# Twelve sorted batches for ten, gates spread by TensorE for gates read from memory, row numbers read for two rounds at once, and every store on ScalarE's queue

## The reference

```
x2   = layernorm(src);  sel = sigmoid(x2 @ sel_w)            # 32 scores
scores, idx = top_k(sel, 4);  gate = scatter of scores       # 28 of 32 gates are zero
h    = relu(einsum("bsd,edh->bseh", x2, keys))
out  = src + einsum("bseh,ehd,bse->bsd", h, values, gate)
```

## Time and profile before

| | |
|---|---|
| median of three executions | 2879.79 us |
| profiled execution, its own time | 2882.87 us |
| its span | 2880.8 us |
| PE busy | 2593.1 us (90%) |
| DVE busy | 1998.2 us (69%) |
| ACT busy | 1546.8 us (54%) |
| POOL busy | 1537.2 us (53%) |
| mean granted TensorE clock | 0.963 |

### The profile page before, as it was taken

The page is one execution under the profiler, slowest core; times in us unless marked ns, Lnnn a source line. Parts: engine busy times, 40 slices in busy tenths (PEclk is TensorE's granted clock), DMA queues, the critical chain, the costliest instruction groups (busy, mean ns, idle before and its releaser), DMA issues. The chain is left out here.

```text
span 2880.8 us, 60293 instructions
## 1 busy us (share of the span) xinstructions
PE 2593.1 (90%) x19992; PEld 1974.2 (69%) x19992; DVE 1998.2 (69%) x4720; ACT 1546.8 (54%) x4605; POOL 1537.2 (53%) x2150
## 2 busy tenths in 40 slices
PE   7999798799979999999886989998999999989699
PEld 5888576588858777777772446665877777769344
DVE  5554587455458999998653556775899999866254
ACT  2333344233359888888510016776988888862000
POOL 4333664432246888887206324554678888740550
PEclk9999899899979999999998989998999999999799
DMA  3700465610022222223264455552222222225454
GB/s 115 312 1 1 112 142 116 261 46 1 1 54 48 54 59 60 60 60 109 67 177 138 174 154 121 107 117 51 45 51 60 60 60 59 55 79 167 147 191 137
DMA packets 225620, 275.90 MB, mean 96 GB/s; under 512 B 26099, under 2 KB 194291, under 8 KB 211987
## 3 DMA queue, kind: packets, MB, share of 16 engines
q1 hardware_dynamic: 190882, 240.03, 30.5%
q0 software_dynamic: 10240, 20.99, 2.6%
q10 hardware_dynamic: 24192, 11.02, 1.3%
HBM read 145.40 MB, written 122.22 MB: 93 GB/s over the span
## 5 line engine op out<-in xcount | busy, mean ns | idle before, releaser
L2803 ACT ACTIVATE f4a_pr<-f4a_sr,f4a_nm 128x256 f32<-128x256 f32 x512 | 239.1, 479 | 50.5 <-DVE f4a_nm L2869 50.2
L2803 ACT ACTIVATE f6a_pr<-f6a_sr,f6a_nm 128x256 f32<-128x256 f32 x512 | 239.0, 479 | 48.0 <-DVE f6a_nm L2869 47.7
L3006 POOL TENSOR_TENSOR f4a_rr<-a5b_room 128x256 f32<-128x256 f32 x256 | 195.3, 763 | 96.1 <-DVE a5b_room L2877 90.1
L3006 POOL TENSOR_TENSOR f6a_rr<-a5b_room 128x256 f32<-128x256 f32 x256 | 195.0, 762 | 87.5 <-DVE a5b_room L2877 81.7
L2005 DVE TENSOR_REDUCE a_nm<-a_sr 128x2 f32<-128x512 f32 x256 | 166.7, 684 | 70.8 <-PE a_sr L1738 69.8
L2877 DVE TENSOR_TENSOR a5b_room<-f4a_ur,f4a_turn 128x512 f32<-128x512 f32 x256 | 174.2, 681 | 35.4 <-PE f4a_ur L2663 33.5
L2877 DVE TENSOR_TENSOR a5b_room<-f6a_ur,f6l_turn 128x512 f32<-128x512 f32 x256 | 174.2, 681 | 30.6 <-PE f6a_ur L2663 27.8
L2869 DVE TENSOR_REDUCE f4a_nm<-f4a_sr 128x2 f32<-128x512 f32 x256 | 174.8, 683 | 20.2 <-PE f4a_sr L2680 19.4
L2678 PE MATMUL f4a_sr<-f4a_pe_hi,f4a_rr_hi 128*128 128x256 f32 x512 | 187.9, 367 | 0.0
L2869 DVE TENSOR_REDUCE f6a_nm<-f6a_sr 128x2 f32<-128x512 f32 x256 | 174.8, 683 | 18.9 <-PE f6a_sr L2680 18.2
L2678 PE MATMUL f6a_sr<-f6l_pe_hi,f6a_rr_hi 128*128 128x256 f32 x512 | 187.5, 366 | 0.0
(11 more groups left out here) (620 smaller groups left out, 8359.4 us busy)
## 6 DMA issues: line engine op xcount, KB each, us to landing
slots<-f_zero SPq DMA_DIRECT2D x84, 512.0 KB, 5.9
f4m_gate<-f4m_gates SPq DMA_DIRECT2D x24, 1024.0 KB
f6m_gate<-f6m_gates SPq DMA_DIRECT2D x24, 1024.0 KB
f4m_xr<-slots SPq DMA_DIRECT2D x112, 64.0 KB, 1.9
f6m_xr<-slots SPq DMA_DIRECT2D x112, 64.0 KB, 1.9
r_scratch<-r_parts SPq DMA_DIRECT2D x32, 192.0 KB, 2.3
all_qs<-r_scratch SPq DMA_DIRECT2D x16, 384.0 KB, 4.8
all_ks<-r_scratch SPq DMA_DIRECT2D x16, 384.0 KB, 6.7
```

The source lines that it names most:

```text
L2803: last = nc.scalar.activation(pr[:, n % 4, x, :], sr.bank(b, n)[:, x * T:(x + 1) * T], ACT.Exp, bias=nm[:, n % SB, x:x + 1], accum_out=zs[ ...
L3006: nc.gpsimd.tensor_tensor(rr[:, hs % RAW, :], tmp[:, hs % 2, 0, :], tmp[:, hs % 2, 1, :], ALU.add)\
```

## The change

- SENT is 12: 24 tiles of tokens are sorted, TILES = 128, ROUNDS = 32, SHARE = 3072, `slots` grows from 86016 to 102400 rows (50 clearing DMAs in each routed feed-forward). Two groups stay for the dense part, N = 64. The table of tiles is made one step later (steps 17 and 18).
- Gates aren't stored and read any more. DVE splits the gates of a group into three bf16 parts (`split`, after rounds 6 and 8), PE turns the three parts together (rounds 9 and 12), and in the dense part PE multiplies a column of ones and zeros (`expert`) by them (`spread`, bf16, 96 rows, 512 columns), which gives the gate of one expert on all partitions; ACT copies it (`take_gate`, 128 x 512), and `weigh` reads the copy. `kept_ps` has two banks instead of three, `gate_ps` two.
- Row and expert numbers are read for two rounds at a time, eight numbers.
- All four stores of a round are ACT's.
- `mix` comes at products 9, 14, 20, 25, 31, 36, 42, 47, 53, 58 and, for the last two, after the loop. The stores of the output come after the rounds in another order on SP.

```diff
-SENT = 10
+SENT = 12
+PARTS = 3
...
-                if it[0] == B and n == 0:
+                if it[0] == B + 1 and n == 0:
                     opening.sort_counts(pe, fill(it, "counts")).then_inc(desk.filled, 1)
...
-                if it[0] == B + 1 and n == 0:
+                if it[0] == B + 2 and n == 0:
                     opening.sort_turn(pe, fill(it, "table")).then_inc(desk.filled, 1)
...
-    LATE, SPLIT, LAG = B - 1, 3, 4
+    LATE, LAG = B - 1, 4
...
-    LOADED, LB, HB, OUT_LAG = 4, 2, 3, 2
+    HB, KB, OUT_LAG = 2, 3, 2
...
-        kept_ps, sum_ps = [spare[:, 0, :], spare[:, 1, :], x_ps[:, :]], [first[:, :], y_ps[:, :], first[:, :]]
+        kept_ps, gate_ps, sum_ps = [spare[:, 0, :], spare[:, 1, :]], [x_ps[:, :], side[:, :]], [first[:, :], y_ps[:, :]]
...
-        TURNS = {7: 0, 10: 1, 13: 2}
-        MIXED = [8 * i + 12 for i in range(SENT)]
+        TURNS = {9: 0, 12: 1}
+        SPLITS = {6: 0, 8: 1}
+        MIXED = [11 * i // 2 + 9 for i in range(SENT)]
...
-            held = [eng.alloc_register(f"{tag}_{name}{r}_{n}") for n in range(QUARTET)]
-            eng.load(held, opening.table[0:1, part * P + r * QUARTET:part * P + (r + 1) * QUARTET])
+            held = [eng.alloc_register(f"{tag}_{name}{r}_{n}") for n in range(2 * QUARTET)]
+            eng.load(held, opening.table[0:1, part * P + r * QUARTET:part * P + (r + 2) * QUARTET])
...
-            def store(r):
-                sp.wait_ge(y_ready, r + 1)
-                for n in range(SPLIT, QUARTET):
-                    sp.dma_start(w.slots[bass.ds(rows[r][n], P), :], y[:, r % YB, n, :]).then_inc(y_out[r % YB], 16)
...
+            def spread(n):
+                g, e = divmod(n, E1)
+                if n >= HB:
+                    pe.wait_ge(gate_ready, n - HB + 1)
+                nc.tensor.matmul(gate_ps[n % HB], expert[:, e:e + 1].to_broadcast([PARTS * E1, P]), gt[:, g, :], start=True, stop=True)\
+                    .then_inc(gate_made, 1)
...
+            spread(0)
             for n in range(N + OUT_LAG):
                 if n < N:
                     keep(n)
+                if n + 1 < N:
+                    spread(n + 1)
                 if n >= OUT_LAG:
                     add(n - OUT_LAG)
...
-                for n in range(SPLIT):
-                    nc.scalar.dma_start(w.slots[bass.ds(rows[n], P), :], y[:, r % YB, n, :]).then_inc(y_out[r % YB], 16)
+                for n in range(QUARTET):
+                    nc.scalar.dma_start(w.slots[bass.ds(rows[r][n], P), :], y[:, r % YB, n, :]).then_inc(y_out[r % YB], 16)
...
+            def take_gate(n):
+                act.wait_ge(gate_made, n + 1)
+                if n >= KB:
+                    act.wait_ge(kept_ready, n - KB + 1)
+                nc.scalar.activation(gate[:, n % KB, :], gate_ps[n % HB], ACT.Copy).then_inc(gate_ready, 1)
...
+            def split(g):
+                dve.wait_ge(opening.gates_ready, (g + 1) * GROUP // TT)
+                nc.vector.tensor_copy(high[:, :, :], opening.gates[g]).then_inc(gate_split, 1)
+                dve.wait_ge(gate_split, 4 * g + 1)
+                nc.vector.tensor_copy(parts[:, g, :, 0:E1], high[:, :, :])
+                nc.vector.tensor_tensor(rest[:, :, :], opening.gates[g], high[:, :, :], ALU.subtract).then_inc(gate_split, 1)
+                dve.wait_ge(gate_split, 4 * g + 2)
+                nc.vector.tensor_copy(middle[:, :, :], rest[:, :, :]).then_inc(gate_split, 1)
+                dve.wait_ge(gate_split, 4 * g + 3)
+                nc.vector.tensor_copy(parts[:, g, :, E1:2 * E1], middle[:, :, :])
+                nc.vector.tensor_tensor(parts[:, g, :, 2 * E1:3 * E1], rest[:, :, :], middle[:, :, :], ALU.subtract).then_inc(gate_split, 1)
+                dve.wait_ge(gate_split, 4 * g + 4)
...
             def weigh(n):
-                q = n // LOADED
                 dve.wait_ge(kept_made, n + 1)
-                if n % LOADED == 0:
-                    dve.wait_ge(gate_in[q % LB], 16 * (q // LB + 1))
-                if n >= HB:
-                    dve.wait_ge(kept_used, n - HB + 1)
...
+                dve.wait_ge(gate_ready, n + 1)
+                if n >= KB:
+                    dve.wait_ge(kept_used, n - KB + 1)
...
-                if then is not None and n in (NT - 4, NT - 2):
-                    for e in range(0, 8) if n == NT - 4 else range(8, E1):
+                if then is not None and n in (13, 17):
+                    for e in range(0, 8) if n == 13 else range(8, E1):
                         then.gpsimd(pool, e)
```

More of the change, by code:

```diff
@@ L2575, in relative_attention @@
         desk = Desk(a.ps("desk", [P, 1, 512]), a.sem("desk_filled"), a.sem("desk_emptied"),
-                    [("count", 5, SENT), ("counts", B, 1), ("table", B + 1, 1), ("rz", 3, B), ("v", 1, B), ("o", 3, B),
-                     ("ends", B, 1), ("xt", 0, B), ("qk", 0, B), ("x2t", 3, B),
+                    [("count", 5, SENT), ("counts", B + 1, 1), ("table", B + 2, 1), ("rz", 3, B), ("v", 1, B), ("o", 3, B),
+                     ("ends", B + 1, 1), ("xt", 0, B), ("qk", 0, B), ("x2t", 3, B),
                      ("sel", 3, B)], 1)
@@ L3099, in load @@
                     all_sent(sp, SENT)
-                rows[r] = registers(sp, "row", r, 0)
+                if r % 2 == 0:
+                    both = registers(sp, "row", r, 0)
+                    rows[r], rows[r + 1] = both[:QUARTET], both[QUARTET:]
                 if r >= XB:
@@ L3132, in store_mixed @@
                 store_tokens(g * GROUP)
-            for r in range(ROUNDS + AHEAD):
-                if r < ROUNDS:
-                    load(r)
-                if r >= AHEAD:
-                    store(r - AHEAD)
-                if r - AHEAD in TURNS:
-                    store_gates(TURNS[r - AHEAD])
-                if r == ROUNDS + 1:
-                    for q in range(LB):
-                        load_gates(q)
+            for r in range(ROUNDS):
+                load(r)
             for n in range(YB):
                 sp.wait_ge(y_out[n], 16 * QUARTET * len(range(n, ROUNDS, YB)))
-            for q in range(LB, N // LOADED):
-                load_gates(q)
-                if out is not None and q >= 10 and q % 4 == 2:
-                    store_mixed((q - 10) // 4)
-                if out is not None and q in (14, 22):
-                    sp.wait_ge(finished, q // 8)
-                    store_tokens(NT + (q // 8 - 1) * GROUP)
             if then is not None:
@@ L3267, in _ @@
         def _(act):
+            rows = {}
             def take_x(r):
@@ L3274, in store @@
             def store(r):
[L3275 removed]
+                if r % 2 == 0:
+                    both = registers(nc.scalar, "row", r, 0)
+                    rows[r], rows[r + 1] = both[:QUARTET], both[QUARTET:]
                 act.wait_ge(y_ready, r + 1)
[L3277 to L3278 removed]
+                for n in range(QUARTET):
+                    nc.scalar.dma_start(w.slots[bass.ds(rows[r][n], P), :], y[:, r % YB, n, :]).then_inc(y_out[r % YB], 16)
             opening.normal(act, LATE)
@@ L3293, in _, with take_sum @@
                     act.wait_ge(side_filled, GATES + TURNS[r])
-                    nc.scalar.activation(gt[:, TURNS[r], :], side[0:E1, :], ACT.Copy).then_inc(side_taken, 1)
-            for g in range(GROUPS):
-                if then is not None and g == GROUPS - 1:
-                    for e in range(E1):
-                        then.scalar(act, e, h_ps[:, :])
+                    nc.scalar.activation(gt[:, TURNS[r], :], side[0:PARTS * E1, :], ACT.Copy).then_inc(side_taken, 1)
+            def take_gate(n):
[3 more added lines that the diff above has]
+                nc.scalar.activation(gate[:, n % KB, :], gate_ps[n % HB], ACT.Copy).then_inc(gate_ready, 1)
+            def take_sum(g):
                 act.wait_ge(kept_used, (g + 1) * E1)
@@ L3302, in _ @@
                 nc.scalar.activation(yt[:, :], sum_ps[g], ACT.Copy).then_inc(sum_ready, 1)
+            for n in range(N):
+                take_gate(n)
+                if n >= E1 and n % E1 == OUT_LAG:
+                    take_sum(n // E1 - 1)
+                if then is not None and n >= N - E1:
+                    then.scalar(act, n % E1, h_ps[:, :])
+            take_sum(GROUPS - 1)
         @block.vector
```

76 lines of the change are left out of this document (37 added, 39 removed).

## The result

The change takes 2854.01 us (median of four runs, 2848.66 to 2857.94) for 2880.14 us of the kernel before beside it: a ratio of 0.9913, 95% interval 0.9892 to 0.9933. That is 26 us gained where 61 were forecast. The profiled execution took 2852.71 us, 30.2 less than that of before.

A forecast was written before the change was run, and what follows sets the result against it. PE, busy 2593.1 of 2880.8 us, was taken as the bound. Dense parts -77, rounds +8 and attention +8 on 2882.9 gave 2822 us, 2819 on the median's scale; range 2753 to 2860.

The forecast's parts named there:

- one stall in each mixture: Dense part: the old stall at the first `mix`, inside POOL's first 40 fetches, comes again; 33 us lost for 31.4.
- POOL keeps up: Dense part, after the stall: `mix` 9.7 or 11.6 us apart, each freed batch of 8 fetches takes 10.0 us.
- the 66 of the sum: Dense parts of both mixtures: the expected stall, 33 us lost in each.
- Rival 2: Dense part: second stall in POOL's long runs, 11 us in f4, at most 3 us at f6's run ends; 2834 us; 25%.
- Rival 3: Dense part: each `mix` begun while POOL fetches starves DVE, 10.9 us each; 2890 us, slower than before; 10%.
- rivals 2 and 4: Rival 4, beside rival 2: rounds stay at 3.12 us or `spread` makes products 2.15; +17 or +28, 2836 to 2847; 10%.
- Rival 1: Dense part: no stall, its cause bound to old code; POOL's fetches then bound it at 131 us; 2756 us; 20%.
- What the change removes: Dense part: 32 products fewer, 55.0 us; the 64 left take 1.93 us; 162.6 for 201.0, 77 less in both.
- The rounds: 32 rounds for 28, PE's pace of 2.66 us for 3.12 from round 9: 97.1 and 97.9 us, +8 in both.
- The attention: More sends and a later table: steps 15 to 18 longer by 0.5, 1.8, 0.9, 0.8; +4 each, +8 in all.
- The rule on who contends: Dense part: by the skill page `weigh`, with one SBUF input, never waits for POOL; the prediction held the trace disagrees.

The follow-up runs named there:

- set 4: The changed kernel, unchanged, run again beside the kernel before (2820.4 us), with no late product: 2758.2 us, ratio 0.9774.
- sets 3 to 5: Three later sets of runs, each with the unchanged kernel before beside it, which took 2822.3, 2820.4 and 2820.7 us.
- the paced kernel: Against the change, GpSimd waits for landing after 12 fetches, then every 8, not before the last 20; `mix` and attention share moved: 2799.4, 2796.8, 2796.2 us.

## Why the prediction was wrong, and where it was right

- **The failed step: one stall in each mixture.** The prediction priced 33 us for the first stall and nothing after it, since "POOL keeps up". The first stall cost 34 and 32 us, as said. But the slow time comes in every long run of fetches, 14 to 16 us into the first and 10 to 14 us into a later one, and the change makes such runs later on: 16 and 24 in f4, three of 16 in f6. POOL does keep up, and just that joins two batches of 8 into one run. Against set 4 the slow time costs 187.6 - 134.3 = 53.3 and 177.4 - 130.1 = 47.3 us, 100.6 for the 66 of the sum: 35 of the missing 40 us. The carried-over term also had the wrong engine: the prediction speaks of "the slow DVE", and it is TensorE's increments that are late. The other 5 are the dense parts without slow time, 134.3 and 130.1 for 129.6 each (162.6 less 33).
- **Rival 2 had the right runs, and too small a size.** It gave 11 us to f4's run of 24 and up to 9 to f6's runs of 16 (4 of them in its 2834 us); by difference the later runs cost 19 us in f4, where the run of 16 is slow too, and 15 in f6. I had put f6's at "at most 3 us at each end", though a run of 20 us that turns slow at 13 has 7 us left and 3 after it.
- **Rival 3 is refuted.** Without any `mix` the stall stays.
- **That 2854 lies in the range is width, not foresight.** No case that was priced gives it: rivals 2 and 4 end at 2839 and 2847, rival 3 is 2890. It is also 9 us lower than the dense parts alone would make it, because the rounds (3) and the rest (6) cost less than their terms.
- **Rival 1 is what happens where the slow time is absent.** It gave 131 us for a dense part and 2756 us; 134.3, 130.1 and 2758.2 were measured. The number is right by luck: its reason was the old code, and the kernel before was 58 us faster in sets 3 to 5 with that code unchanged (there is no trace of it from there). What decides is the run.
- **What the change removes was right.** Set the slow time aside on both sides: dense parts of 172.8 and 168.0 us before become 134.3 and 130.1, 76.4 us less. The like term of the sum is 80 (169.6 for 129.6, twice, the stalls left out). The product takes 1.94 us for the 1.93 that the earlier trace rows gave.
- **The rounds were right.** 96.1 us each for 97.1 and 97.9 (99.3 and 94.6 in set 4). From the ninth on they are 2.72 and 2.77 us apart for 2.66. PE's waits for loads before its turns fell to 19.1 us in 4 waits in f4 and 19.0 in 4 in f6, from 39.0 in 20 and 30.9 in 17. Reads and store undone together cost 16 us (2774.5 for 2758.2) for the 20 expected; which of the two it is was not tried. ACT was not what PE waited for.
- **The attention was right in three steps and half of its size.** Step 15 (1297.80 to 1334.35) takes 36.55 us for 36.10, step 16 (to 1369.53) 35.18 for 33.31, step 17 (to 1398.93) 29.40 for 28.49: +0.5, +1.9, +0.9 for +0.5, +1.8, +0.9. But from the first mark to the first turn of the rounds f4 and f6 grow by 2.0 and 1.9 us for 4 each: step 14 shrinks by 0.6, and the 0.8 of step 18 doesn't show.
- **The rule on who contends.** The prediction weighed the Trainium skill, SBUF — State Buffer, "Who interferes with whom", by which `weigh` never waits for GpSimd. It held that the trace disagrees. It doesn't: `weigh` waits for TensorE's increments, starts 0.02 to 0.03 us after them and takes its 0.69 us, also at the gap of 11.92 us in the kernel without `mix`. Without slow time the trace agrees through 96 fetches. So the slow time is no case of that rule, and something else comes with GpSimd's fetches.

**What stays open.** What holds TensorE's increments back, why it was there for some sets of runs and not for others, and whether bytes, rows or instructions fill what the onsets suggest: the runs with half the bytes and half the rows all fell where it was absent. So did all runs of the paced kernel. Of the kernels tried, the one that waits after every 8 fetches (2810 us) beats the kernel before and the change where the slow time is present; where it is absent no complete one beats the change itself (2758 us), and pacing costs 39 us. Whether one with fewer pauses is good in both was not tried.

## What to carry to other kernels

When a stall has no name in the profile ("issue", "remote"), look first which other engines are late in it and which goes on at once: the late ones may all wait for the signals of the one that looks well. Then ask whether it is in every run before pricing it: run the kernel before in several sets, and change one thing that should move it. Price such a stall by the stretch of the neighbour's work that it lies in, and look for every such stretch that the change creates, not only for the old one. One late start after a long neighbour is no loss while the next catches up: compare the length of the whole series.

## What the runs showed of the hardware

- TensorE's semaphore increments can come late beside a long series of GpSimd's indirect DMAs: from 14 to 16 us into a first unbroken run, ever later (1.1, 8.3, 19.0, 25.4 us), to 3 to 6 us after its end, while the fetches keep their 0.94 us and VectorE's and ScalarE's own signals reach TensorE in 0.05 us. Within a run of 40 fetches one product then takes 8 to 14 us for 1.94, in runs of 16 up to 8. Pauses of 2.3 us after every 8 fetches avoid it. It was present or absent over whole sets of runs, worth 58 us to the kernel before.
- A fetch of 64 rows takes GpSimd 0.90 us, one of 128 rows 0.94, and one of 128 half rows 0.95.
- TensorE loses clock over the waits: the same 348 matmuls are busy 149.1 us at a granted clock of 0.84 and 130.2 us at 0.98, which can be at most 19 of the 53 us that the slow time costs f4.
